# Layer-norm statistics spread over attention steps on VectorE, and a shorter wait between two layers, in a fused transformer kernel

## The chip, the cores and the metric

The kernel runs on one core of one Trainium2 chip. The metric is the device time in microseconds (us) of one execution. TensorE multiplies matrices, VectorE does element-wise work and reductions, ScalarE exponentials and copies, GpSimd masks and indirect transfers, and SyncE starts most DMA transfers. Each engine works through its own instructions in their order and waits on semaphores for the others.

## What is computed

The input x has 16 sequences of 256 tokens of 128 features. Four parts follow each other, each added to x:

```python
x = x + attn_a(layernorm(x))   # 16 heads of 8, causal softmax
x = x + ffn(layernorm(x))      # 8 experts of 128 -> 512 -> 128, the best 2 for each token
x = x + attn_b(layernorm(x))   # 16 heads of 8, no mask, a scale and shift worked out for each head
x = x + ffn(layernorm(x))
```

The layer norm subtracts the mean of a token's 128 features and divides by sqrt(variance + 1e-5).

## The kernel before, in words

x stays in on-chip memory as 32 blocks of 128 tokens, two blocks to a sequence. The kernel has four stages: attention "A", a feed-forward stage, attention "B", a second feed-forward stage. "Layer A" and "layer B" are called l = 0 and l = 1 in the code.

**An attention layer is a pipeline of steps j.** Step j (`pipeline`, `pe_step`, `dve_step` and so on) projects sequence j, computes the scores of sequence j-2 for their row maxima, the transposed scores and exponentials of sequence j-3, and the output of sequence j-4. Each step goes through 16 slots h, one for each head. In slot h TensorE writes the scores of head h (L355, in layer A with a mask matmul L386) into one of two banks psS, and VectorE reduces the bank to the row maxima (mx, L671). TensorE's scores of slot h wait for the maximum of slot h-2, `after(pe, s["mx"], 16 * bS + h - 1)`, so VectorE can be at most about two slots late before TensorE stands still. Beside the maxima VectorE has other duties in fixed slots: xs, the normalised input of step j, in slot 0; the lower part of a maximum in slots 2 and 10; the softmax division in slots 5 and 12; the residual in slots 9 and 15; in layer A splits in slots 11 and 14.

**Hooks put further work between the slots.** `dve_beside` issues work for VectorE at the end of a given slot. Part of it are the layer-norm statistics of a group of blocks, by `dve_ln_at`. It cuts them into one call for each value of its argument h: count/2 calls with two `bn_stats` each (one for each block), two calls with half of the `bn_aggr` each, and a last call, the root (`dve_ln_root`): 13 small instructions, each of which waits for the one before, that give 1/sqrt(variance + eps) by an integer seed and three Newton steps. VectorE does nothing else during the root. Where `dve_ln_at` is called:

- layer A, step 5: blocks 16 to 31 of the input, for the inputs xs from step 8 on
- layer A, step 13: blocks 0 to 15, for the feed-forward stage
- layer B, step 7: blocks 16 to 31, for the inputs xs from step 8 on
- layer B, step 14: blocks 0 to 15, for the second feed-forward stage
- step 18 of both layers and the feed-forward stages, which stay as they are

In layer B `dve_combine_1` also adds the experts' outputs of blocks 16 to 31 to x, four blocks at a time: in slot 4 of steps 4, 5 and 6, and in slot 2 of step 7.

**A feed-forward stage** goes through 71 tiles of 128 tokens (`tile_loop`). The result of a tile is copied by VectorE to ysb (L1417), and a DMA started by SyncE stores it to eo in DRAM. GpSimd gathers the rows of eo later, and waits itself for the stores (`pool_gather`). After the first feed-forward stage TensorE and ScalarE call `ffn_over` ahead of layer B, which begins with step 2, since the projections of sequences 0 and 1 were made beside the last tiles.

Of the kernel before, what the change touches and what calls it, by code (L numbers as in the profile page):

```python
# [23 lines left out]
HALF = NBLK // 2  # L24
SIZE = (16, 16)
BASE = (0, SIZE[0])
QUADS = (SIZE[0] // 4, SIZE[1] // 4)
TILES = 2 * NBLK + E - 1
# [40 lines left out]
def build(nc, A, out):  # L69
    with ExitStack() as ctx:  # L70
# [35 lines left out]
        part = sb("part", [P, 2, 3, T], BF16)  # L106
# [82 lines left out]
        s_lnA = sem("s_lnA")  # L189
# [3 lines left out]
        s_ln = [sem("s_ln0"), sem("s_ln1"), sem("s_ln2"), sem("s_ln3")]  # L193
# [4 lines left out]
        s_lnB = sem("s_lnB")  # L198
# [696 lines left out]
        def tiles_done(p, l, count):  # L895

            return 16 * (l * ((TILES + 1 - p) // 2) + (count + 1 - p) // 2)

        def ffn_over(eng, l):

            eng.wait_ge(f_sem["y"], TILES * (l + 1))
            for i in range(2):
                eng.wait_ge(f_st[i], tiles_done(i, l, TILES))

        LG_COPIES = (0, 1, 3, 4)

# [725 lines left out]
        def dve_beside(l):  # L1632
            n = 2 * l

            def hook(dve, j, h):
                x1 = (LA, LB)[l].s["x1"]
                if l == 0 and j == 1 and h == 1:
                    dve.wait_ge(s_xrest, 16)
                    dve_ln_stats(dve, 4, HALF, s_lnA)
                    dve.wait_ge(s_lnA, 2)  # L1640
                if l == 0 and j == 5 and h == 0:
                    dve.wait_ge(s_xlast, 16)
                if l == 0 and j == 5:
                    dve_ln_at(dve, h, HALF, HALF, s_lnA, 3)
                if l == 0 and j == 1 and h == 15:
                    dve.wait_ge(s_mset, 2 * RING)
                    nc.vector.memset(half[0:1, 0, :], -0.5).then_inc(s_half, 1)
                    nc.vector.memset(half[0:1, 1, :], 1.5).then_inc(s_half, 1)
                    dve.wait_ge(s_cst, 16)
                    nc.vector.memset(onesb[:], 1.0).then_inc(s_half, 1)  # L1650
                    nc.vector.tensor_copy(triu[:], cst[:, CST_TRIU:CST_TRIU + P]).then_inc(s_half, 1)
                if l == 1 and (j, h) in ((4, 4), (5, 4), (6, 4), (7, 2)):
                    dve_combine_1(dve, 0, j - 4)
                if l == 1 and (j, h) == (2, 12):
                    dve_route_part(dve, 1, 2)
                if l == 1 and j == 7:
                    dve_ln_at(dve, h, SIZE[0], SIZE[1], s_lnB, 3)
                if l == 0 and j == 13:
                    if h == 0:
                        dve.wait_ge(x1, HALF)  # L1660
                    dve_ln_at(dve, h, 0, HALF, s_ln[0], 1)
                if l == 0 and j == 14:
                    if h % 4 == 1:
                        dve_tokens(dve, 0, h - 1, h + 3)
                if l == 0 and j == 15:
                    if h == 9:
                        dve_logits(dve, 0, 0, QUADS[0], 1)
                    if h in (10, 11):
                        dve_route_part(dve, 0, h - 10)
                    if h == 15:  # L1670
                        dve_counts(dve, 0)
                if l == 0 and j == 16 and h < 4:
                    dve_route_part(dve, 0, h + 4)
                if l == 1 and j == 14:
                    if h == 0:
                        dve.wait_ge(x1, SIZE[0])
                    dve_ln_at(dve, h, 0, SIZE[0], s_ln[2], 1)
                if l == 1 and j == 16 and h in (8, 9):
                    if h == 8:
                        dve_logits(dve, n, 0, QUADS[0], LG_COPIES[n] + 1)  # L1680
                    dve_route_part(dve, n, h - 8)
                if l == 1 and j == 16 and h == 11:
                    dve_counts(dve, n)
                if l == 1 and j == 16 and 12 <= h < 16:
                    dve_route_part(dve, n, h - 8)
                if j == 18 and h == 15:
                    dve_route_part(dve, n, 8)
                    dve_route_part(dve, n, 2)
                if j == 18:
                    if h == 0:  # L1690
                        dve.wait_ge(x1, NBLK - 4)
                    dve_ln_at(dve, h, SIZE[0], NBLK - 4 - SIZE[0], s_ln[n + 1], 1)
                    if 10 <= h < 14:
                        dve_tokens(dve, n + 1, SIZE[0] + 3 * (h - 10), SIZE[0] + 3 * (h - 9))
                if j == 19 and h == 10:
                    dve_logits(dve, n + 1, 0, QUADS[1] - 1, LG_COPIES[n + 1] + 1)
                    dve_pick(dve, n + 1, 0, 0, NBLK - 4 - BASE[1])
                if j == 19 and h == 13:
                    dve_pick(dve, n + 1, 1, 0, NBLK - 4 - BASE[1])
                if l == 0 and j == 18 and h == 15:  # L1700
                    dve_setup(dve, LB)
            return hook
# [155 lines left out]
```

## Time and profile before

| | |
|---|---|
| median of 3 runs | 1166.69 us (1163.05 to 1168.38) |
| profiled execution | 1166.68 us, of which the span of the trace is 1164.9 us |
| TensorE matmuls busy | 1029.9 us (88%) |
| VectorE busy | 755.5 us (65%) |
| ScalarE busy | 672.4 us (58%) |
| GpSimd busy | 525.5 us (45%) |
| TensorE's granted clock, mean | 0.92 |

A span is the time from the first to the last event of the trace. The granted clock is 1.00 at 2.4 GHz and 0.50 at 1.2 GHz; a value between them is the mean of a stretch that has both. A shared number of busy engines says little here: the stages have different limits, so the prediction reads single steps.

A step is taken from the start of VectorE's xs (L583) to the next one. In a row of a window stand: its bounds, its length, then for TensorE's matmuls, TensorE's weight loads, VectorE, ScalarE and GpSimd the busy time with the number of instructions in brackets, then TensorE's granted clock, the DMA engines' share and GB/s. In a row of a timeline stand: start, duration, engine, line, operation, what is written and read, shapes, count, and in square brackets the idle time of the engine just before it and what ended it. Instructions of one engine overlap a little.

### The profile page before, as it was taken

What the parts mean: (1) busy time and instruction counts of PE and PEld (TensorE: products, weight loads), DVE (VectorE), ACT (ScalarE), POOL (GpSimd) and SP (SyncE); (2) the same over time, 40 slices, a digit from 0 to 9 for tenths busy, and PEclk for the clock granted to TensorE, in tenths of its full rate; (3) what the DMA queues carried; (4) which work ended last, traced back from release to release, by engine and by line L of the source; (5) the groups of instructions that cost most, each with busy time, mean ns of one, the idle gap of its engine ahead of it and who ended that gap; (6) DMA issues with size and microseconds to landing.
All of it is one profiled execution on the core that took longest, in us unless ns stands there. A gap on an engine that the chain in (4) does not pass through costs nothing.

```text
span 1164.9 us, 28879 instructions
## 1 busy us (share of the span) xinstructions
PE 1029.9 (88%) x9290; PEld 716.6 (62%) x9290; DVE 755.5 (65%) x2322; ACT 672.4 (58%) x1399; POOL 525.5 (45%) x980
## 2 busy tenths in 40 slices
PE   2998999897989999999798979999888799999990
PEld 1444555453468989999443434444443589999990
DVE  4687778877777333456777888888877663334442
ACT  2365676663644545556277858897757445455550
POOL 2243444332742610344687736455736436004455
PEclk9998999996989999999778979998888899999995
DMA  6446544562235878887544323343221469778873
GB/s 152 104 114 138 116 110 99 151 181 57 54 118 174 271 233 236 260 255 236 125 111 104 101 56 85 89 107 84 65 49 44 130 191 280 227 242 256 272 225 109
DMA packets 201723, 175.03 MB, mean 150 GB/s; under 512 B 19812, under 2 KB 160616, under 8 KB 201576
## 3 DMA queue, kind: packets, MB, share of 16 engines
q1 hardware_dynamic: 193384, 156.41, 49.1%
q0 software_dynamic: 8192, 16.79, 4.8%
q8 instruction: 76, 1.25, 0.5%
q14 instruction: 71, 0.58, 0.2%
HBM read 122.99 MB, written 50.14 MB: 149 GB/s over the span
## 4 chain that ended last, share of the span: by engine, by line
PE 60%; DVE 11%; issue 6%; POOL 5%; DMA 4%; SPq 3%; ACT 1%; POOLq 0%; ACTq 0%; DVEq 0%
PE psS L1358 9%; PE psT L1365 9%; PE psO L321 8%; PE psS L355 7%; PE psO L1381 4%; PE psN L1381 4%; DVE mx L671 4%; PE psS L386 3%; PE psT L363 3%; POOL xn L1259 3%; PE psM L276 2%; PE psN L328 2%; DMA eo<-ysb 2%; PE psN L337 1%; PE psM L1346 1%
## 5 line engine op out<-in xcount | busy, mean ns | idle before, releaser
L671 DVE TENSOR_REDUCE mx<-psS 128x3 f32<-128x384 f32 (+1 forms) x512 | 311.4, 617 | 119.5 <-PE psS L386 61.8
L355 PE MATMUL psS<-kst,qst 48*128 48x256 bf16 (+1 forms) x1024 | 201.7, 286 | 46.4 <-DVE mx L671 33.2
L558 ACT ACTIVATE pT<-psT,scb 128x512 f32<-128x512 f32 x256 | 193.9, 777 | 43.2 <-PE psT L363 40.7
L363 PE MATMUL psT<-qst,kst 50*128 50x256 bf16 (+1 forms) x1024 | 194.7, 278 | 4.6 <-DMA qst<-scr_m 2.2
L1422 DVE TENSOR_TENSOR hT<-sg,psT 128x512 f32<-128x512 f32 x142 | 97.5, 686 | 154.4 <-PE psT L1365 127.7
L1245 POOL DMA_INDIRECT xg<-xn,slot x128 | 123.1, 962 | 131.3 <-DVE ysb L1417 72.1
L1358 PE MATMUL psS<-xTt,wgc 128*128 128x128 f32 x1136 | 153.7, 279 | 5.7 <-issue 5.3
L355 PEld LDWEIGHTS psS<-kst,qst 48*128 48x128 bf16 x1024 | 66.2, 97 | 146.0 <-DVE mx L671 68.2
L1365 PE MATMUL psT<-xTt,wuc 128*128 128x128 f32 x1136 | 152.2, 278 | 1.5 <-DMA wuc<-in_L_ffn_Wu 1.4
L790 POOL TENSOR_SCALAR_AFFINE_SELECT pT<-pT 128x256 f32<-128x256 f32 x224 | 90.6, 412 | 133.0 <-ACT pT L553 131.8
L553 ACT ACTIVATE pT<-psT 128x384 f32<-128x384 f32 x256 | 122.9, 490 | 46.1 <-PE psT L363 35.9
L1358 PEld LDWEIGHTS psS<-xTt,wgc 128*128 128x128 f32 x1136 | 140.0, 194 | 9.2 <-issue 8.5
L1365 PEld LDWEIGHTS psT<-xTt,wuc 128*128 128x128 f32 x1136 | 140.0, 194 | 2.3 <-DMA wuc<-in_L_ffn_Wu 2.3
L321 PE MATMUL psO<-pT,vp 128*32 128x256 f32 (+1 forms) x2048 | 141.0, 399 | 0.4 <-ACT pT L558 0.3
L1259 POOL DMA_INDIRECT pT<-eo,slot x64 | 60.4, 944 | 175.9 <-DVE ysb L1417 105.7
L1401 ACT ACTIVATE sg<-psS 128x512 f32<-128x512 f32 x142 | 84.7, 596 | 83.0 <-PE psS L1358 82.9
L1409 ACT ACTIVATE wdc<-wd 128x512 f32 x142 | 89.5, 630 | 52.1 <-issue 48.7
L321 PEld LDWEIGHTS psO<-pT,vp 128*32 128x32 f32 x2048 | 57.6, 118 | 55.5 <-issue 29.1
L1392 ACT ACTIVATE xTt<-psM 128x128 f32<-128x128 f32 x142 | 39.3, 277 | 70.5 <-PE psM L1346 70.3
L386 PE MATMUL psS<-trib,identb 128*128 128x256 bf16 x256 | 77.5, 303 | 0.0
L1381 PE MATMUL psN<-wdc,hT 128*128 128x128 f32 x576 | 76.2, 275 | 1.0 <-DVE ysb L1417 1.0
L1381 PE MATMUL psO<-wdc,hT 128*128 128x128 f32 x560 | 74.3, 276 | 0.5 <-DVE ysb L1417 0.5
(225 smaller groups left out, 1595.1 us busy)
## 6 DMA issues: line engine op xcount, KB each, us to landing
wgc<-in_L_ffn_Wg SPq DMA_DIRECT2D x142, 256.0 KB, 3.1
wuc<-in_L_ffn_Wu SPq DMA_DIRECT2D x142, 256.0 KB
scr_part<-part SPq DMA_DIRECT2D x128, 128.0 KB, 2.1
qst<-scr_part SPq DMA_DIRECT2D x64, 192.0 KB, 3.7
kst<-scr_part SPq DMA_DIRECT2D x64, 192.0 KB, 4.7
xin<-xg SPq DMA_DIRECT2D x142, 64.0 KB
eo<-ysb SPq DMA_DIRECT2D x142, 64.0 KB
scr_part<-part SPq DMA_DIRECT2D x32, 192.0 KB, 1.9
```

The source lines that it names most:

```text
L321: last = nc.tensor.matmul(psO[q // 2][32 * i:32 * i + 32, o0 + dst[0]:o0 + dst[1]], vp[r][:, kb, h, :], pT[:, h % 8, src[0]:src[1]], start ...
L355: return nc.tensor.matmul(ps[:, c0:c0 + n], q_[r64, t, q0], k_[r64, t, 0:n], start=(half == 0), stop=True, skip_group_check=True)
L363: return nc.tensor.matmul(ps[:, c0:c0 + T - q0], k_[m64, t, half * P:half * P + P], q_[m64, t, q0:T], start=(half == 0 or not L.causal), s ...
L386: last_s = nc.tensor.matmul(psS[par][:, 0:3 * P].rearrange("p (a k) -> p a k", a=3)[:, 0:3:2, :], identb[:], trib[:].unsqueeze(1).to_broad ...
L553: nc.scalar.activation(pT[:, g % 8, 0:cols], psT[g % 2][:, 0:cols], ACT.Exp, scale=float(HD) ** -0.5).then_inc(s["exp"], 1)
L558: nc.scalar.activation(pT[:, g % 8, 0:cols], psT[g % 2][:, 0:cols], ACT.Exp, scale=scb[r][:, 0, i:i + 1], bias=scb[r][:, 1, i:i + 1]).then ...
L671: nc.vector.tensor_reduce(mx3[:, u, 0:n, pos:pos + 1].rearrange("p a b -> p (a b)"), psS[h % 2][:, 0:kcols(L)].rearrange("p (a k) -> p a k ...
L1245: nc.gpsimd.indirect_dma_start(xg, bass.IndirectOffsetOnAxis(ap=slot[g][:, i, k:k + 1], axis=0), xn[:, BASE[g] + k, :], None).then_inc(r_s ...
L1358: last = nc.tensor.matmul(psS[p][:, cols], wgc[n % FETCH][:, cols], xTt[n % FETCH][:], start=True, stop=True, skip_group_check=True)
L1365: last = nc.tensor.matmul(psT[p][:, cols], wuc[n % FETCH][:, cols], xTt[n % FETCH][:], start=True, stop=True, skip_group_check=True)
L1381: last = nc.tensor.matmul(psY[p][:, 0:P], hT[(n0 + k - 2) % FETCH][:, hb, :], wdc[(n0 + k - 2) % FETCH][:, hb * P:(hb + 1) * P], start=(hb ...
L1422: nc.vector.tensor_tensor(out=hT[(n0 + k) % FETCH][:].rearrange("p a c -> p (a c)"), in0=sg[p][:], in1=psT[p][:], op=ALU.mult).then_inc(f[ ...
```

## The change

**Statistics.** The calls of `dve_ln_at` are dealt over two steps, and in layer B, blocks 16 to 31, over two groups of eight blocks with a root each:

| statistics | before | after |
|---|---|---|
| layer A, blocks 16 to 31 | step 5, slots 0 to 10 | `bn_stats` in the even slots of step 4, `bn_aggr` in slots 0 and 1 and the root in slot 2 of step 5 |
| layer A, blocks 0 to 15 | step 13, slots 0 to 10 | the same way in steps 12 and 13 |
| layer B, blocks 16 to 23 | step 7, slots 0 to 10 (16 blocks) | `bn_stats` in slots 0, 4, 8, 12 of step 6, the rest in slots 0 to 2 of step 7 |
| layer B, blocks 24 to 31 | (same) | `bn_stats` in slots 0, 4, 8, 12 of step 9, the rest in slots 0 to 2 of step 10 |
| layer B, blocks 0 to 15 | step 14, slots 0 to 10 | even slots of step 13, slots 0 to 2 of step 14 |

The last call of `dve_combine_1` moves from slot 2 of step 7 to slot 4 of step 8.

**The wait.** `ffn_over` no longer waits for the stores of the tiles (f_st), only for the copies to ysb (y). TensorE's and ScalarE's work of layer B doesn't read what the stores write; GpSimd's gathers keep their own waits.

```diff
         def ffn_over(eng, l):
 
             eng.wait_ge(f_sem["y"], TILES * (l + 1))
-            for i in range(2):
-                eng.wait_ge(f_st[i], tiles_done(i, l, TILES))
...
-                if l == 0 and j == 5 and h == 0:
+                if l == 0 and j == 4 and h == 0:
                     dve.wait_ge(s_xlast, 16)
-                if l == 0 and j == 5:
-                    dve_ln_at(dve, h, HALF, HALF, s_lnA, 3)
+                if l == 0 and j == 4 and h % 2 == 0:
+                    dve_ln_at(dve, h // 2, HALF, HALF, s_lnA, 3)
+                if l == 0 and j == 5 and h < 3:
+                    dve_ln_at(dve, HALF // 2 + h, HALF, HALF, s_lnA, 3)
...
-                if l == 1 and (j, h) in ((4, 4), (5, 4), (6, 4), (7, 2)):
-                    dve_combine_1(dve, 0, j - 4)
+                if l == 1 and (j, h) in ((4, 4), (5, 4), (6, 4), (8, 4)):
+                    dve_combine_1(dve, 0, min(j - 4, 3))
...
-                if l == 1 and j == 7:
-                    dve_ln_at(dve, h, SIZE[0], SIZE[1], s_lnB, 3)
-                if l == 0 and j == 13:
-                    if h == 0:
-                        dve.wait_ge(x1, HALF)
-                    dve_ln_at(dve, h, 0, HALF, s_ln[0], 1)
+                for part, (first, times) in enumerate(((6, 3), (9, 4))):
+                    lo, count = SIZE[0] + part * SIZE[1] // 2, SIZE[1] // 2
+                    if l == 1 and j == first and h % 4 == 0:
+                        dve_ln_at(dve, h // 4, lo, count, s_lnB, times)
+                    if l == 1 and j == first + 1 and h < 3:
+                        dve_ln_at(dve, count // 2 + h, lo, count, s_lnB, times)
+                if l == 0 and j == 12 and h == 0:
+                    dve.wait_ge(x1, HALF)
+                if l == 0 and j == 12 and h % 2 == 0:
+                    dve_ln_at(dve, h // 2, 0, HALF, s_ln[0], 1)
+                if l == 0 and j == 13 and h < 3:
+                    dve_ln_at(dve, HALF // 2 + h, 0, HALF, s_ln[0], 1)
...
-                if l == 1 and j == 14:
-                    if h == 0:
-                        dve.wait_ge(x1, SIZE[0])
-                    dve_ln_at(dve, h, 0, SIZE[0], s_ln[2], 1)
+                if l == 1 and j == 13 and h == 0:
+                    dve.wait_ge(x1, SIZE[0])
+                if l == 1 and j == 13 and h % 2 == 0:
+                    dve_ln_at(dve, h // 2, 0, SIZE[0], s_ln[2], 1)
+                if l == 1 and j == 14 and h < 3:
+                    dve_ln_at(dve, SIZE[0] // 2 + h, 0, SIZE[0], s_ln[2], 1)
```

VectorE's instructions from slot 12 of step 4 of layer A to slot 2 of step 5, after the change (mx is a maximum, bn_stats appear as BN_STATS):

```order
L934 BN_STATS bn<-x 128x6 x2
L671 TENSOR_REDUCE mx<-psS 128x3
L705 TENSOR_TENSOR vp<-psM,b_wideA 128x16x8 x2
L671 TENSOR_REDUCE mx<-psS 128x3
L627 TENSOR_TENSOR part<-rest,part 128x2x256
L934 BN_STATS bn<-x 128x6 x2
L671 TENSOR_REDUCE mx<-psS 128x3
```

Before the change the same place had no BN_STATS; the first of them stood behind the xs of step 5:

```order
L583 TENSOR_SCALAR xs<-x,mean_rstd 128x128 x2
L936 BN_STATS bn<-x 128x6 x2
L671 TENSOR_REDUCE mx<-psS 128x3
L936 BN_STATS bn<-x 128x6 x2
L671 TENSOR_REDUCE mx<-psS 128x3
```

So two pairs more stand ahead of the last maxima of step 4 (a third stands in slot 10).

VectorE's instructions from slot 1 to slot 3 of step 7 of layer B, before the change (L1289 adds the experts' outputs):

```order
L936 BN_STATS bn<-x 128x6 x2
L671 TENSOR_REDUCE mx<-psS 128x2
L633 SCALAR_TENSOR_TENSOR mrow<-psN,neg_shift,mrow 8x256
L1289 SCALAR_TENSOR_TENSOR x<-xn,wgt,x 128x128 x8
L936 BN_STATS bn<-x 128x6 x2
L671 TENSOR_REDUCE mx<-psS 128x2
```

And the same slots after it, in step 7 and again in step 10, where nothing of the kind stood before (the root begins with L880):

```order
L583 TENSOR_SCALAR xs<-x,mean_rstd 128x128 x2
L939 BN_AGGR mean_rstd<-bn 128x2 x4
L671 TENSOR_REDUCE mx<-psS 128x2
L688 COPY scb<-psM 128x32
L690 COPY neg_shift<-psM 8x2
L939 BN_AGGR mean_rstd<-bn 128x2 x4
L671 TENSOR_REDUCE mx<-psS 128x2
L633 SCALAR_TENSOR_TENSOR mrow<-psN,neg_shift,mrow 8x256
L880 TENSOR_SCALAR nwt<-mean_rstd 128x8
```

The root now stands between the maxima of slots 2 and 3, where the experts' outputs were added before, instead of between those of slots 10 and 11.

## Rows read from the trace of the kernel before

**Rows 1.** The page of the kernel before: busy time of TensorE.

```profile
PE 1029.9 (88%) x9290; PEld 716.6 (62%) x9290; DVE 755.5 (65%) x2322; ACT 672.4 (58%) x1399; POOL 525.5 (45%) x980
```

**Rows 2.** Windows, one per step; columns as described above.

```profile
62.62:78.53 15.91, 15.39 (x174) 8.14 (x172) 12.57 (x33) 11.23 (x27) 7.10 (x17) 1.00 0.45 102
78.53:99.16 20.63, 16.98 (x174) 8.55 (x172) 18.87 (x78) 11.61 (x27) 7.08 (x17) 0.92 0.74 173
212.74:233.89 21.15, 17.50 (x172) 8.53 (x171) 19.01 (x79) 11.62 (x27) 7.09 (x17) 0.85 0.66 188
647.97:668.69 20.72, 18.13 (x172) 8.62 (x168) 17.13 (x50) 16.06 (x33) 14.00 (x32) 0.92 0.41 101
668.69:697.63 28.94, 22.10 (x160) 9.69 (x160) 23.72 (x94) 15.95 (x32) 11.13 (x28) 0.72 0.25 61
697.63:716.13 18.50, 18.03 (x184) 8.92 (x176) 15.01 (x41) 16.50 (x34) 9.88 (x28) 0.98 0.39 89
786.32:803.86 17.54, 16.94 (x172) 8.35 (x168) 14.84 (x41) 15.72 (x33) 9.84 (x28) 1.00 0.41 93
803.86:829.89 26.03, 22.00 (x172) 9.96 (x168) 21.46 (x86) 16.27 (x33) 16.09 (x36) 0.74 0.26 63
```

**Rows 3.** Timeline of VectorE, end of step 4, layer A.

```profile
72.22 0.56 DVE L671 TENSOR_REDUCE mx<-psS 128x3 f32<-128x384 f32 x1 [0.84 <-PE psS L386]
```

**Rows 4.** Timeline of TensorE, idle time in brackets, layer A.

```profile
77.92 0.23 PE L355 MATMUL psS<-kst,qst 48*128 48x128 bf16 x1 [0.45 <-DVE mx L671]
...
80.88 0.23 PE L355 MATMUL psS<-kst,qst 48*128 48x128 bf16 x1 [0.21 <-DVE mx L671]
...
93.69 0.23 PE L355 MATMUL psS<-kst,qst 48*128 48x128 bf16 x1 [2.67 <-DVE mx L671]
```

**Rows 5.** Timeline of VectorE, steps 7 and 14, layer B.

```profile
671.72 2.29 DVE L1289 SCALAR_TENSOR_TENSOR x<-xn,wgt,x 128x128 f32<-128x128 f32 x8
...
804.37 0.47 DVE L936 BATCH_NORM_STATS2 bn<-x 128x6 f32<-128x128 f32 x2
...
815.77 0.63 DVE L941 BATCH_NORM_AGGREGATE mean_rstd<-bn 128x2 f32<-128x6 f32 x8
...
819.60 0.15 DVE L880 TENSOR_SCALAR nwt<-mean_rstd 128x16 f32<-128x16 f32 x1
...
822.29 1.29 DVE L671 TENSOR_REDUCE mx<-psS 128x2 f32<-128x512 f32 x2
```

**Rows 6.** Timeline of TensorE, steps 6, 7 and 14, layer B.

```profile
656.06 0.33 PE L333 MATMUL psN<-ident,on 128*128 128x128 f32 x1 [2.26 <-DVE on L643]
...
675.18 0.39 PE L355 MATMUL psS<-kst,qst 48*128 48x256 bf16 x1 [2.61 <-DVE mx L671]
...
805.49 0.28 PE L355 MATMUL psS<-kst,qst 48*128 48x256 bf16 x1 [0.61 <-DVE mx L671]
...
806.63 0.28 PE L355 MATMUL psS<-kst,qst 48*128 48x256 bf16 x1 [0.39 <-DVE mx L671]
```

**Rows 7.** Windows over stretches of the lower granted clock.

```profile
94.33:97.74 3.41, 3.41 (x29) 1.51 (x21) 2.64 (x8) 2.36 (x6) 0.81 (x2) 0.50 0.61 178
...
674.60:681.40 6.80, 6.22 (x37) 2.58 (x37) 4.72 (x17) 2.38 (x5) 3.55 (x17) 0.50 0.64 116
807.70:818.00 10.30, 10.03 (x62) 3.90 (x61) 8.05 (x38) 5.43 (x12) 7.01 (x21) 0.50 0.41 81
```

**Rows 8.** Timeline of VectorE: the last copy of the first feed-forward stage.

```profile
563.90 0.28 DVE L1417 COPY ysb<-psN 128x128 f32<-128x128 f32 x1
```

**Rows 9.** Timeline of TensorE: the first scores of layer B.

```profile
566.09 0.61 PE L355 MATMUL psS<-kst,qst 48*128 48x256 bf16 x4 [3.76 <-DMA eo<-ysb]
```

**Rows 10.** The chain that ended last, at the same place.

```profile
564.37 1.63 DMA eo<-ysb
```

**Rows 11.** Tile kst from 550 to 575 us: DMA issues to it.

```profile
L819 SPq DMA_DIRECT2D kst<-scr_part x4: 432/472/536, 556.1 to 572.4; - x4
DMA to landing us min/median/max: 4.1/4.8/5.4
```
## The prediction

> **What bounds the kernel now.** The page comes first: TensorE's matmuls are busy for 88% of the span [rows 1]. Then the windows of single steps, which are what the change touches. A step without statistics takes 15.91 us in layer A and 17.54 us in layer B, and TensorE is busy for all but 0.52 and 0.60 us of them; VectorE idles 3.3 and 2.7 us. The steps with statistics are longer: +4.72 us (step 5, layer A), +5.24 us (step 13), +11.40 us (step 7, layer B, with the experts' outputs), +8.49 us (step 14); step 8 is 0.96 us over [rows 2]. So at most some 31 us are at stake, and the question is what of them the new places give back.
>
> Two losses make up each of these. One is TensorE's idle time: length less busy time rises by 3.13 us in step 5, 3.13 us in step 13, 6.24 us in step 7 and 3.43 us in step 14. The other is that the same matmuls take longer: +1.59, +2.11, +5.16 and +5.06 us, with a granted clock of 0.92, 0.85, 0.72 and 0.74 [rows 2]. The timeline of TensorE shows where the idle time is. In step 5 one wait on a maximum has 2.67 us, and it ends when the root does; the statistics in slots 0 and 1 left only 0.21 us [rows 4]. In layer B they left 0.61 and 0.39 us [rows 6], and a half-clock stretch of 10.3 us followed; after the 2.67 us wait one of 3.4 us, after the 2.61 us wait of step 7 one of 6.8 us [rows 6, 7].
>
> **Cost of the pieces.** Two bn_stats take 0.47 us (0.4 us taken, since neighbours overlap), eight bn_aggr 0.63 us, the root 822.29 - 819.60 = 2.69 us, the experts' outputs 2.29 us [rows 5]. The root is one uninterrupted piece before and after, and has the same 13 instructions for 8 blocks as for 16. That is my main argument: the change spreads what was cheap and keeps whole what was dear, and layer B, blocks 16 to 31, gets a second root. What would a root cost in slot 2? Step 7 shows it: there the experts' outputs and one pair of statistics, 2.29 + 0.4 = 2.69 us, stood between the maxima of slots 2 and 3, and TensorE waited 2.61 us [rows 5, 6]. A root at slot 2 is the same length at the same place.
>
> **What a half clock costs.** From windows: in step 14 the clock of 0.74 means 2 x 0.26 x 26.03 = 13.5 us at half, for 5.06 us of longer matmuls, 0.37 us for each. In step 7 it is 2 x 0.28 x 28.94 = 16.2 us for 5.16 us, 0.32 for each; in step 5 it is 3.3 us for 1.59 us, 0.48 for each [rows 2]. I use 0.32 to 0.37 in layer B. The Trainium skill (TensorE: Matmul & The Clock Gate, section Terms) gives the loss as throttled time x (1 - K/N), that is 0.5 for each microsecond at half; the trace is below it where VectorE's waits overlap, and by the rule step 14 would have lost 6.8 us to the clock instead of 5.1.
>
> **Layer A, steps 4 and 5.** In step 4 VectorE starts the maximum of slot 10 after an idle 0.84 us, and from there works without a pause into the next step, where TensorE waits 0.45 us for it [rows 3, 4]. Pairs in slots 0 to 8 fall into idle time. Those of slots 10, 12 and 14 lie in the unbroken run, so 3 x 0.4 = 1.2 us go to TensorE's wait (bounds 0 and 1.2). A wait of 0.45 + 1.2 us in one place may bring a half-clock stretch of its own: 0 or 1.6 us, 0.8 taken. Step 5: two half groups of bn_aggr in slots 0 and 1 are 2 x 0.23 us longer than the pairs they replace, the root costs 2.67 us as before and a stretch at half clock 1.6 us; I take the 4.7 us of before again (4.0 to 5.5). Sum of both: +2.0 us.
>
> **Layer A, steps 12 and 13.** The same, but the half clock after the root was already longer there (0.85 against 0.92 [rows 2]), so I add no second stretch: +1.2 us (0 to 3).
>
> **Layer B, steps 6 to 10.** Before: 11.40 + 0.96 = 12.4 us over the normal steps. After: step 6 has pairs at slots 0 and 4, where VectorE was late already (a 2.26 us wait [rows 6]), +0.8 us. Step 7: waits of 0.61 + 0.39 + 2.61 us [rows 6], of which a normal step has some 0.4, so 3.2 us, and 6.8 us of half clock [rows 7] x 0.32 = 2.2 us: 5.4 us. Step 8 gets the experts' outputs in slot 4, as step 6 has them: 20.72 - 17.54 = 3.2 us [rows 2] (2 to 3.2, since part of step 6's is GpSimd's gathering). Step 9: one pair exposed, 0.4 us. Step 10: a root as in step 7, 5.4 us. Sum 15.2 us against 12.4: +2.8 us (-2 to +7).
>
> **Layer B, steps 13 and 14.** Eight pairs, 3.2 us, go into a step in which VectorE idles 2.7 us [rows 2]. Slots 0 and 2 cost 0.6 us; of slots 10 to 14 I let 0.8 us (0 to 1.2) arrive in step 14. There: 0.8 + 0.61 + 0.39 + 2.61 us, 0.5 us since bn_aggr is longer than a pair, less 0.4: 4.5 us. Half clock between 2.2 us (6.8 us as in step 7) and 3.8 us (10.3 us x 0.37 [rows 7]), 3.0 taken. 0.6 + 4.5 + 3.0 = 8.1 us against 8.49: -0.4 us (-3 to +2).
>
> **The boundary.** VectorE's last copy starts at 563.90 and takes 0.28 us [rows 8], so it ends at 564.18; the scores start at 566.09 after 3.76 us of idle time, ended by the store [rows 9], which in the chain takes 1.63 us [rows 10]. Without the wait the scores start about 1.8 us earlier. What else must be there: kst, issued from 556.1 on and landed at most 5.4 us later [rows 11], even with half a microsecond for its second piece 562.0 at the latest. Behind it VectorE's xs and GpSimd's chain start with the same step, so the gain stays: -1.8 us (-1.9 to 0). The Trainium skill (DMA: Bandwidth & Descriptors, "Anatomy of one DMA") puts a transfer's fixed cost at about 2.0 us; by that the gain would be 2.2 us, the trace shows less.
>
> **Sum.** -1.8 + 2.0 + 1.2 + 2.8 - 0.4 = +3.8 us on the profiled execution of 1166.68 us, which lies at the median of the runs (1166.69): 1170.5 us. GpSimd's normalising in step 14 starts earlier, but nothing of the next step waits for it.
>
> **Rivals.**
> 1. Shorter stretches: every root brings only 3.4 us of half clock (1.3 us), as in step 5, and none at the step ends. Against my sum that saves 0.8 + 0.3 in steps 4 and 5, 2.1 - 1.3 in step 13, 2 x 0.9 in steps 7 and 10 and 3.0 - 1.3 in step 14, 5.4 us: 1165 us. For it: with statistics spread, TensorE enters the root without small waits before it. Against it: bn_aggr sits there instead. 25%.
> 2. Clearly faster: TensorE holds its full clock through the roots. Then of the four places only idle time is left: 1.2 + 3.1 - 4.7, the same with 5.2, 0.8 + 3.2 + 2.3 + 0.4 + 3.2 - 12.4, 0.6 + 4.5 - 8.5, and the boundary: -0.4 - 0.9 - 2.5 - 3.4 - 1.8 = -9 us, 1158 us. Against it: the waits of 2.67 and 2.61 us, and even those of 0.61 and 0.39 us together, had a half-clock stretch behind them [rows 4, 6, 7]. It decides if TensorE's waits stay under that of 0.61 + 0.39 us. 17%.
> 3. Slower: each root of layer B brings 10.3 us of half clock and each step end in layer A one more stretch. That is 0.8 + 1.6 us more in layer A, 2 x 1.6 in steps 7 and 10 and 0.8 in step 14 of layer B, +6.4 us: 1177 us. It decides once lags of the step end and the root fall together, as in steps 13 and 14. 18%.
> 4. The wait at the boundary is only replaced (by ScalarE, GpSimd or the clock): 1172 us, with the forecast. Its share of the forecast's 40% is a fourth.
>
> **How the numbers follow.** 40% for 1167 to 1173, with 1170.5 the likeliest; the others as given. Two in ten left out: 1157 to 1178 us. A measurement here can tell about 0.5%, 5.8 us, from no change. Faster than 1160.9: rival 2 and a little of rival 1, 0.20. Slower than 1172.5: rival 3 and the upper part of the forecast, 0.27. Same: 0.53.
>
> **What would show it.** Right: waits of about 2.6 us on a maximum in slot 5 of steps 5 and 13 (A), 7, 10 and 14 (B); a wait of 1 to 2 us at the end of steps 4 and 12; step 10 near 23 us; scores of layer B under 0.3 us behind the last copy. Wrong: steps 5, 7, 10 and 14 with a clock near 1.00, or waits there well below 2.6 us, or step 13 of layer B at 17.5 us.

## The result: 0.66% slower

The changed kernel takes 1172.64 us (median of 5 runs, 1169.91 to 1174.10) against 1164.48 us for the kernel before in the same comparison (5 runs, 1163.05 to 1168.38). The ratio is 1.0066, with a 95% interval of 1.0043 to 1.0088, so it is slower by 5 to 10 us. The prediction had 1170.5 us, a range of 1157 to 1178 us and 27% for slower by over 0.5%. Its profiled execution took 1169.91 us, with a span of 1168.2 us; that is its fastest run, so the single trace shows less than the medians do.

The page after, its first lines (span, then busy time of each engine):

```profile
span 1168.2 us, 28898 instructions
PE 1028.0 (88%) x9290; PEld 716.3 (61%) x9290; DVE 757.7 (65%) x2335; ACT 673.2 (58%) x1399; POOL 526.3 (45%) x980
```

TensorE is busy as long as before [rows 1]. VectorE has 13 instructions more, one root. The loss is in how the steps fit together, and the windows by step show it (bounds, length, then busy times, and the third number from the end is TensorE's granted clock). Layer A, steps 4, 5, 12, 13 and 14, then layer B, steps 6, 7, 8, 9, 10, 13 and 14:

```profile
62.04:79.14 17.10, 15.85 (x174) 8.22 (x172) 15.38 (x50) 11.19 (x27) 7.51 (x17) 1.00 0.43 106
79.14:99.88 20.74, 16.89 (x174) 8.64 (x172) 16.18 (x62) 11.57 (x27) 7.16 (x17) 0.92 0.63 147
195.99:213.06 17.07, 15.82 (x174) 8.22 (x172) 15.37 (x49) 11.19 (x27) 7.49 (x17) 1.00 0.44 106
213.06:234.40 21.34, 18.33 (x174) 9.18 (x172) 16.46 (x62) 11.57 (x27) 7.17 (x17) 0.84 0.58 151
234.40:255.35 20.95, 17.71 (x178) 9.36 (x177) 17.09 (x49) 12.44 (x29) 7.27 (x17) 0.92 0.68 175
647.04:667.20 20.16, 18.12 (x172) 8.87 (x168) 18.65 (x57) 16.08 (x33) 13.94 (x32) 0.92 0.39 102
667.20:689.90 22.70, 19.13 (x172) 9.20 (x168) 17.75 (x62) 16.13 (x33) 9.90 (x28) 0.85 0.33 79
689.90:709.79 19.89, 18.02 (x172) 8.63 (x168) 17.07 (x49) 16.07 (x33) 9.89 (x28) 0.91 0.34 83
709.79:728.18 18.39, 16.89 (x172) 8.43 (x168) 16.47 (x49) 15.81 (x33) 9.86 (x28) 1.00 0.34 89
728.18:751.11 22.93, 19.03 (x172) 9.05 (x168) 17.75 (x62) 16.13 (x33) 9.89 (x28) 0.85 0.29 72
786.22:807.09 20.87, 18.71 (x173) 8.88 (x169) 17.72 (x58) 16.23 (x33) 9.91 (x28) 0.92 0.34 78
807.09:830.13 23.04, 18.93 (x172) 9.17 (x168) 18.36 (x70) 15.95 (x33) 15.70 (x36) 0.85 0.31 71
```

Against [rows 2]: step 7 of layer B fell from 28.94 to 22.70 us and step 14 from 26.03 to 23.04 us. But the step ahead of each group now costs something (17.10 for 15.91 us in layer A, 20.87 for 17.54 us in layer B), step 5 of layer A is no shorter (20.74 for 20.63 us), and step 10 of layer B, where nothing stood, is 22.93 us long.

The timeline of TensorE after the change has the waits behind the roots, which now stand in slot 2 (idle time in brackets). Layer A, end of step 4, step 5 and step 14; layer B, first scores, steps 7, 10 and 14:

```profile
78.53 0.23 PE L355 MATMUL psS<-kst,qst 48*128 48x128 bf16 x1 [0.84 <-DVE mx L671]
...
85.77 0.23 PE L355 MATMUL psS<-kst,qst 48*128 48x128 bf16 x1 [2.66 <-DVE mx L671]
...
243.88 0.34 PE L363 MATMUL psT<-qst,kst 50*128 50x256 bf16 x1 [1.65 <-DMA qst<-scr_m]
...
565.16 0.61 PE L355 MATMUL psS<-kst,qst 48*128 48x256 bf16 x4 [1.85 <-DVE ysb L1415]
...
673.62 0.39 PE L355 MATMUL psS<-kst,qst 48*128 48x256 bf16 x1 [2.17 <-DVE mx L671]
...
734.60 0.39 PE L355 MATMUL psS<-kst,qst 48*128 48x256 bf16 x1 [2.50 <-DVE mx L671]
...
814.12 0.39 PE L355 MATMUL psS<-kst,qst 48*128 48x256 bf16 x1 [2.14 <-DVE mx L671]
```

2.66 us in step 5 is the 2.67 us of [rows 4], eight slots earlier; step 13 of layer A has such a wait of 2.50 us. The boundary wait fell from 3.76 [rows 9] to 1.85 us and is now ended by VectorE's copy. The wait of 1.65 us in step 14 was not there before.

### The profile page after: what moved, and what is told of

Same layout as the page of the kernel before. It is cut to its first block, busy times and chain, and to the rows that moved or that the text cites. A ratio compares the mean times of both kernels' runs of the same rounds, so it can differ in the third digit from the quotient of the medians.

```text
span 1168.2 us, 28898 instructions
## 1 busy us (share of the span) xinstructions
PE 1028.0 (88%) x9290; PEld 716.3 (61%) x9290; DVE 757.7 (65%) x2335; ACT 673.2 (58%) x1399; POOL 526.3 (45%) x980
## 4 chain that ended last, share of the span: by engine, by line
PE 59%; DVE 13%; POOL 9%; issue 8%; DMA 6%; SPq 3%; ACT 2%; POOLq 0%; ACTq 0%; DVEq 0%
PE psS L1356 9%; PE psT L1363 9%; PE psO L321 8%; PE psS L355 7%; PE psO L1379 4%; PE psN L1379 4%; DVE mx L671 4%; POOL xn L1257 4%; PE psS L386 3%; PE psT L363 3%; PE psM L276 3%; POOL prow L745 2%; PE psN L328 2%; POOL part L758 1%; PE psN L337 1%
## 5 line engine op out<-in xcount | busy, mean ns | idle before, releaser
L355 PE MATMUL psS<-kst,qst 48*128 48x256 bf16 (+1 forms) x1024 | 199.1, 282 | 50.2 <-DVE mx L671 39.7
L558 ACT ACTIVATE pT<-psT,scb 128x512 f32<-128x512 f32 x256 | 194.4, 778 | 46.2 <-PE psT L363 43.5
L363 PE MATMUL psT<-qst,kst 50*128 50x256 bf16 (+1 forms) x1024 | 192.2, 275 | 5.5 <-DMA qst<-scr_m 2.7
L553 ACT ACTIVATE pT<-psT 128x384 f32<-128x384 f32 x256 | 123.0, 491 | 53.1 <-PE psT L363 43.6
```

Of the source, the lines that this page charges most:

```text
L355: return nc.tensor.matmul(ps[:, c0:c0 + n], q_[r64, t, q0], k_[r64, t, 0:n], start=(half == 0), stop=True, skip_group_check=True)
L363: return nc.tensor.matmul(ps[:, c0:c0 + T - q0], k_[m64, t, half * P:half * P + P], q_[m64, t, q0:T], start=(half == 0 or not L.causal), s ...
L553: nc.scalar.activation(pT[:, g % 8, 0:cols], psT[g % 2][:, 0:cols], ACT.Exp, scale=float(HD) ** -0.5).then_inc(s["exp"], 1)
L558: nc.scalar.activation(pT[:, g % 8, 0:cols], psT[g % 2][:, 0:cols], ACT.Exp, scale=scb[r][:, 0, i:i + 1], bias=scb[r][:, 1, i:i + 1]).then ...
```

## The experiments

"Below" and "above" are taken from the ratio to the kernel before, run on the same chip in the same comparison. 1% is 11.7 us.

**1. Only the shorter wait.**

```diff
             eng.wait_ge(f_sem["y"], TILES * (l + 1))
-            for i in range(2):
-                eng.wait_ge(f_st[i], tiles_done(i, l, TILES))
```

> Only the shorter wait at the boundary; the statistics stay as before. Theory T (the terms of the prediction): the scores of layer B start some 2 us earlier and the gain stays, so 1.8 to 2.2 us below the kernel before. Rival R (the loss is at the boundary: starting earlier costs more later, in steps 2 to 6 or in the second feed-forward stage): equal to the kernel before, or above it by up to 5 us.

1161.90 us against 1164.96 us, ratio 0.9971 (0.9953 to 0.9988): 1.4 to 5.5 us faster. Theory T holds, R falls. From the xs of sequence 1 to that of step 2 it takes 27.3 us in this trace and 26.9 in the changed kernel's, 28.7 to 29.1 us in the traces that keep the wait: 1.8 us less by the means. In the changed kernel the first scores start 0.06 us behind VectorE's last copy.

**2. Only the statistics.** The changed kernel with the two lines of the wait put back.

> Only the statistics dealt over the steps; the boundary waits for the stores as before. Theory T: all of the loss is here, so about 2 us above the changed kernel, that is 8 to 11 us above the kernel before. Rival R: between the kernel before and the changed one, 0 to 4 us above before.

1176.01 us, ratio 1.0099 (1.0069 to 1.0128): 8 to 15 us slower. The dealt statistics are the loss, and the wait takes some 2 to 4 us off it (1.8 us by the traces, 3.8 us by the two ratios).

**3. Only layer A.** The kernel before with the dealt calls of steps 4, 5, 12 and 13.

> Only the two groups of layer A are dealt over two steps (4 and 5, 12 and 13). Theory T: +1.2 us for each of steps 4 and 12 and what step 14 lost in the changed kernel's trace (2.2 us), less 1.3 us in step 6: 2.5 to 3.5 us above the kernel before. Rival R: no loss in layer A that lasts, within 1 us of the kernel before.

1170.08 us, ratio 1.0041 (1.0019 to 1.0064): 2 to 7 us slower, about half of the loss; rival R falls. Its step 5 shows how much the clock adds by chance:

```profile
78.55:102.36 23.81, 20.83 (x174) 9.64 (x172) 16.36 (x62) 11.81 (x27) 7.24 (x17) 0.72 0.53 128
```

The same instructions took 20.74 us at a clock of 0.92 in the changed kernel and 23.81 us at 0.72 here; TensorE idles less (2.98 against 3.85 us), its matmuls take 3.9 us longer. So two traces of the same instructions can differ by 3 us in one step, and the steps of a single trace have to be read with that in mind.

**4. Only blocks 16 to 31 of layer B.**

> Only blocks 16 to 31 in layer B are dealt as in the change: two groups, two roots, the last experts' outputs in step 8. Theory T: step 7 loses about 6 us of its length, steps 8, 9 and 10 gain 1.4, 0.8 and 5.4, so 0.8 to 2.8 us above the kernel before, and step 10 is near 23 us. Rival R: a second root of eight blocks is cheap, step 10 under 19 us and the whole some 4 us below the kernel before.

1169.92 us, ratio 1.0042 (1.0023 to 1.0060): 3 to 7 us slower, where I expected 0.8 to 2.8 us; step 10 is 22.96 us long. A root of 8 blocks is not cheap, and rival R falls. The excesses of experiments 3 and 4, 0.41% and 0.42%, add to most of the 0.99% of experiment 2.

The next four ran on another chip, on which the kernel before takes 1229.08 us (33 runs, 1223.62 to 1238.06), mostly because its feed-forward stages are longer (301.0 and 365.1 us in the trace of experiment 6, 276.4 and 333.1 us in that of the kernel before). Ratios hold within that comparison. Steps of layer A and steps 9 to 13 of layer B are as long as in the traces so far where they have the same work (15.88 and 17.55 us). The changed kernel did not run on this chip: where it is the measure, its ratio of 1.0066 is taken over from the first comparison.

**5. The roots of the changed kernel in four pieces.**

```diff
-                if l == 0 and j == 5 and h < 3:
-                    dve_ln_at(dve, HALF // 2 + h, HALF, HALF, s_lnA, 3)
+                if l == 0 and j == 5 and h in (0, 1, 2, 4, 6, 8):
+                    dve_ln_at(dve, HALF // 2 + (0, 1, 2, 4, 6, 8).index(h), HALF, HALF, s_lnA, 3, True)
```

and the same in steps 13 of layer A and 7, 10 and 14 of layer B. A piece is the start with its integer seed (3 instructions), or one Newton step (3), the last one with the copy.

> The changed kernel, with the five roots of its dealt groups cut into four pieces of 3 to 4 instructions, in slots 2, 4, 6 and 8 instead of all in slot 2. Theory T (the root's unbroken 2.7 us late in the slots is what TensorE waits for; a piece of 0.65 us falls into VectorE's idle time): each of the five waits of 2.1 to 2.7 us and most of the half clock behind it go, some 3.5 us each, so 14 to 20 us below the changed kernel, and steps 5 (layer A) and 10 (layer B) are under 18.5 and 20 us. Rival S (VectorE's added work costs the same wherever it stands): within 3 us of the changed kernel.

Ratio 0.9993 (0.9973 to 1.0014). The changed kernel stands at 1.0066, so the pieces take off some 8 us, not 14 to 20. In layer A the waits on the root are gone as theory T has it: steps 5 and 13 are 17.86 us long at full clock. But step 6 then took 18.86 us, against 17.01 us in the changed kernel, with a wait of 1.45 us on a transfer (qst<-scr_m), so over steps 4 to 6 only 1.0 us of the 2.9 us is left; experiment 10 comes back to this. In layer B steps 7 and 10 stay long (the rows are step 5 of layer A, then 7 and 10 of layer B):

```profile
79.14:97.00 17.86, 15.69 (x174) 8.18 (x172) 16.12 (x63) 11.43 (x27) 7.07 (x17) 1.00 0.72 164
...
701.72:722.13 20.41, 16.82 (x172) 8.15 (x168) 19.24 (x63) 16.47 (x33) 9.89 (x28) 1.00 0.33 80
761.78:784.46 22.68, 19.33 (x172) 8.96 (x168) 19.27 (x63) 16.58 (x33) 9.92 (x28) 0.85 0.32 73
```

VectorE is busy for 19.27 us in step 10, where the changed kernel had 17.75 us with the same work: two instructions of the root take 1.15 and 0.90 us there, and 0.17 us elsewhere. Experiment 8 shows what runs beside them. Steps 7 and 10 have the same waits of TensorE to 0.03 us (0.64, 0.40, 0.50 and 1.55 us in step 7, which has one of 0.20 us more), and yet step 7 kept the full clock and step 10 did not.

**6. The roots of the kernel before in four pieces, in slots 10 to 13.**

> The kernel before, with only its four roots cut into the same four pieces, in slots 10, 11, 12 and 13 of the same step; everything else as before. Theory T (the place counts as much as the length: behind slot 10 VectorE works without a pause anyway): TensorE still waits for most of the 2.7 us, in several smaller waits, so 0 to 5 us below the kernel before. Rival U (only the unbroken length counts): 10 to 15 us below the kernel before.

Ratio 1.0000 (0.9974 to 1.0025). Theory T holds, rival U falls. TensorE's waits in step 5 are now several: 0.43, 0.84 and

```profile
96.22 0.21 PE L355 MATMUL psS<-kst,qst 48*128 48x128 bf16 x1 [1.56 <-DVE mx L671]
```

which is 2.8 us together, against one of 2.67 us [rows 4]. Behind slot 10 VectorE has no idle time to hide the root in, and cutting it there gives little in layer A: steps 5 and 13 take 19.91 and 20.01 us, 0.7 and 1.1 us less than in [rows 2]. Cutting it and placing it in slots 2 to 8 gives 3 us in a step (experiment 5). Steps 7 and 14 of layer B took 25.67 and 23.23 us in this trace, 3.3 and 2.8 us less than in [rows 2], and the whole still gains nothing. There is no trace of the kernel before on this chip, so where that is lost again stays open.

**7. The pairs of bn_stats in slots 1 to 8 instead of the even slots** (2 to 9 in layer B, step 13).

```diff
-                if l == 0 and j == 4 and h % 2 == 0:
-                    dve_ln_at(dve, h // 2, HALF, HALF, s_lnA, 3)
+                if l == 0 and j == 4 and 1 <= h <= 8:
+                    dve_ln_at(dve, h - 1, HALF, HALF, s_lnA, 3)
```

> The changed kernel, with the eight pairs of bn_stats of steps 4 and 12 (layer A) in slots 1 to 8 instead of the even slots, and those of step 13 (layer B) in slots 2 to 9; aggregation and root as in the change. Theory T (the pairs of slots 10, 12 and 14 lie in the unbroken run and cost 0.4 us each, those of slots 3 to 9 fall into idle time): steps 4 and 12 are back at 15.9 us, step 13 at 17.5 to 18.5 us, 3 to 6 us below the changed kernel. Rival S: no difference.

Ratio 1.0016 (1.0000 to 1.0033), against 1.0066 for the change: about 6 us less. Theory T holds. Steps 4 and 12 of layer A and 13 of layer B:

```profile
62.22:78.44 16.22, 15.57 (x175) 8.14 (x172) 15.37 (x50) 11.24 (x27) 7.14 (x17) 1.00 0.45 104
195.67:211.81 16.14, 15.52 (x174) 8.16 (x172) 15.37 (x50) 11.24 (x27) 7.11 (x17) 1.00 0.41 101
826.62:844.72 18.10, 16.72 (x172) 8.24 (x168) 17.73 (x58) 15.77 (x33) 9.83 (x28) 1.00 0.39 90
```

VectorE's busy time is that of the changed kernel (15.37 and 17.73 us); only the slots differ, and 0.9 us a step in layer A and 2.8 us in layer B are gone. The pairs in slot 0 and from slot 10 on were the cost; the run moved both and does not part them.

**8. Everything in the idle slots.** The kernel before with the shorter wait, and all four groups in slots 3 to 9: for layer A

```diff
+            if j == first and 3 <= h < 9:
+                dve_ln_at(dve, h - 3, lo, count, done, times, True)
+            if j == first + 1 and h in (3, 4, 6, 8):
+                dve_ln_at(dve, 6 + (3, 4, 6, 8).index(h), lo, count, done, times, True)
+            if j == first + 2 and h in (3, 5, 7, 8):
+                dve_ln_at(dve, 10 + (3, 5, 7, 8).index(h), lo, count, done, times, True)
```

with first = 4 and 11; blocks 0 to 15 of layer B so from step 12 on, blocks 16 to 31 in two groups in steps 6, 7 and 10, 11, and `dve_combine_1` in halves in slots 4 and 7 of steps 4, 5, 8 and 9.

> The kernel before with the shorter wait of the change, and all statistics and roots of the four groups dealt over two or three steps, with nothing in slots 0 to 2 and 10 to 15: pairs and bn_aggr in slots 3 to 9, the roots in four pieces in slots 3 to 9 of a later step, the experts' outputs of steps 4, 5, 8 and 9 in two halves in slots 4 and 7. Theory T: the steps with statistics are within 1 us of the normal ones (15.9 and 17.5 us); of the 30 us that they had over them 20 to 27 go, and 2 us at the boundary: 1136 to 1145 us. Rival S: the same work, so at most the 3 us of the boundary.

Ratio 0.9924 (0.9895 to 0.9953): 6 to 13 us faster, not the 22 to 29 us that I expected with the boundary. Steps 4, 5, 12 and 13 of layer A are at 16.01, 17.11, 16.22 and 16.32 us, but others are not. Step 5 of layer B takes 29.22 us, where the other three traces of this chip have 25.5 to 28.0 us; why is open. Two losses can be read. First, steps 6 and 14 of layer A take 20.03 and 22.05 us and wait for the same transfer, for 2.48 us in step 6 and in step 14 so:

```profile
237.86 0.28 PE L363 MATMUL psT<-qst,kst 50*128 50x256 bf16 x1 [2.79 <-DMA qst<-scr_m]
```

Second, step 11 of layer B takes 21.43 us. VectorE's last piece of the root and GpSimd's splits of the projections at the same time, from the two timelines:

```profile
787.18 0.16 DVE L937 SCALAR_TENSOR_TENSOR nwt<-nwt 128x8 f32<-128x8 f32 x1
787.37 1.01 DVE L938 TENSOR_TENSOR nwt<-nwt 128x8 f32<-128x8 f32 x1
788.42 0.17 DVE L939 SCALAR_TENSOR_TENSOR nwt<-nwt 128x8 f32<-128x8 f32 x1
788.62 0.90 DVE L941 COPY mean_rstd<-nwt 128x8 f32<-128x8 f32 x1
```

```profile
787.18 1.18 POOL L758 TENSOR_TENSOR rest<-qk,part 128x512 f32<-128x512 f32 x1
788.44 1.05 POOL L758 TENSOR_TENSOR part<-rest,zero 128x512 bf16<-128x512 f32 x1
```

The 8-column multiplication took 1.01 us, not 0.17, and ended at 788.38, where GpSimd's instruction ended at 788.36; the copy ended at 789.52 with GpSimd's next one at 789.49. The maximum behind the copy came late, and TensorE waited 1.62 us for it. Experiments 9 to 12 take these two losses apart, 9 to 11 on a chip where the kernel before takes 1163.95 us, 12 on one where it takes 1165.33 us.

**9. The pieces ahead of the split,** in slots 3, 5, 6 and 7. The edit does this in both layers, though it is meant for layer B.

> The kernel of the idle slots, with the root's pieces of layer B in slots 3, 5, 6 and 7, ahead of GpSimd's four split instructions, instead of up to slot 9. Theory V (a small VectorE instruction that begins while GpSimd splits is held until GpSimd's instruction ends, 1.0 us instead of 0.17): the two long instructions in each of steps 7, 11 and 14 and the waits of 1.4 to 1.6 us behind them go, 1.5 to 4 us for each step, 4 to 10 us below the kernel of the idle slots, that is 13 to 20 us below the kernel before. Rival (chance, or the pieces themselves): steps 7 and 11 stay above 20 us.

1149.61 us, ratio 0.9899 (0.9867 to 0.9931). This is the faster chip, so the comparison with experiment 8 goes by ratios: 0.25% less, with intervals that overlap; it is not shown as a gain, and the 4 to 10 us expected did not come. Nor did the run test theory V, since what held VectorE did not go: GpSimd began its split with the last piece in slot 7, and one multiplication took 1.13 us and the copy 1.01 us in each of the three steps. Steps 7, 11 and 14 took 22.22, 19.38 and 19.43 us, against 20.45, 21.43 and 19.05 us in experiment 8. Steps 7 and 11 have the same instructions and nearly the same waits (0.39 and 1.51 us, 0.38 and 1.51 us); the clock makes the difference:

```profile
660.74:682.96 22.22, 19.45 (x172) 9.13 (x168) 18.79 (x54) 16.29 (x33) 9.87 (x28) 0.85 0.40 100
737.40:756.78 19.38, 16.58 (x172) 8.06 (x168) 18.60 (x54) 15.86 (x33) 9.87 (x28) 1.00 0.36 84
```

The last run moves that piece.

**10. The same, with SyncE's large transfers spread.**

```diff
-            if j == 5:
-                for e in (2 * point, 2 * point + 1):
+            if j in (3, 4, 5, 6) and point == 3:
+                for e in (2 * (j - 3), 2 * (j - 3) + 1):
...
-            if j in (13, 14):
+            if 7 <= j <= 14 and point == 3:
                 sp.wait_ge(s_zero, 1)
-                part8 = 4 * (j - 13) + point
+                part8 = j - 7
```

> The same kernel, and the large transfers that SyncE starts beside layer A are spread: the eight loads of the experts' weights over steps 3 to 6 instead of step 5, the eight zero fills of the token buffer over steps 7 to 14 instead of 13 and 14, always at the end of SyncE's step. Theory W (what steps 5 and 13 gain comes back in steps 6 and 14, because the exchange of the row maxima waits behind these transfers): TensorE's waits of 1.5 to 2.8 us on that exchange in steps 6 and 14 go, another 4 to 8 us. Rival: the exchange is slow for another reason, no difference.

1141.62 us, ratio 0.9812 (0.9785 to 0.9840), 10 us below experiment 9 by the ratios, with intervals that don't meet. Steps 5, 6, 13 and 14 of layer A, which took 17.17, 19.10, 16.71 and 21.78 us in experiment 9:

```profile
78.73:94.95 16.22, 15.42 (x174) 8.12 (x172) 14.42 (x53) 11.25 (x27) 7.13 (x17) 1.00 0.57 140
94.95:111.45 16.50, 15.58 (x174) 8.21 (x172) 15.04 (x46) 11.36 (x27) 7.11 (x17) 1.00 0.49 116
207.29:223.70 16.41, 15.44 (x174) 8.13 (x172) 15.13 (x46) 11.25 (x27) 7.09 (x17) 1.00 0.49 135
223.70:241.48 17.78, 16.19 (x177) 8.87 (x176) 16.85 (x50) 12.27 (x29) 7.26 (x17) 1.00 0.49 119
```

Together 66.9 us against 74.8. The wait on the exchange of the row maxima (qst<-scr_m) was 1.56 us in step 6 and 2.48 us in step 14; it is 0.41 us in step 6 now and gone in step 14, and so is the half clock. Theory W holds: these transfers were what the exchange waited for. Whether it stood behind them in SyncE's queue or shared the DMA engines with them no run parts.

**11. The change as it was, with the same spread of the transfers.**

> The changed kernel with the same spread of the transfers and nothing else. Theory W: step 14 comes down from 21 us by 1.5 to 3 us and step 6 by some 1 us, so 2 to 5 us below the changed kernel, 3 to 6 us above the kernel before. Rival: as the changed kernel, 8 us above the kernel before.

1171.71 us, ratio 1.0063 (1.0034 to 1.0092): no difference from the change is seen, where I expected 2 to 5 us; the two intervals leave room for a gain of some 4 us. Steps 13 and 14 of layer A:

```profile
215.54:239.34 23.80, 20.83 (x174) 9.62 (x172) 16.38 (x63) 11.82 (x27) 7.20 (x17) 0.72 0.34 86
239.34:257.11 17.77, 16.18 (x177) 8.88 (x176) 16.84 (x49) 12.26 (x29) 7.26 (x17) 1.00 0.46 116
```

Step 14 gained 3.2 us and lost its wait on the exchange, as expected, but step 13 with its root had a clock of 0.72 and lost 2.5 us. Step 6 did not gain (18.92 us). Whether the clock of step 13 follows from the moved transfers or is the chance seen in experiments 3 and 9 is open; one trace does not tell it.

**12. The last piece in slot 6** (slots 3, 4, 5 and 6), again in both layers.

> The kernel with the moved transfers, and the root's four pieces of layer B in slots 3, 4, 5 and 6: the last piece stood in slot 7, where GpSimd's split began with it. Theory V: no small VectorE instruction of 1.0 us is left in steps 7, 11 and 14, TensorE's waits of 1.5 us behind them go, and these steps fall from 19.4 to 20.8 us to 18 to 19 us: 3 to 6 us less, 22 to 28 us below the kernel before. Rival: pieces in four neighbouring slots bring waits of their own, no gain or a loss of up to 3 us.

1143.86 us against 1165.33 us, ratio 0.9823 (0.9799 to 0.9847): no gain over experiment 10 is seen, where I expected 3 to 6 us. What held VectorE is gone, as expected; the last piece in step 7:

```profile
663.48 0.16 DVE L937 SCALAR_TENSOR_TENSOR nwt<-nwt 128x8 f32<-128x8 f32 x1
663.67 0.17 DVE L938 TENSOR_TENSOR nwt<-nwt 128x8 f32<-128x8 f32 x1
663.87 0.17 DVE L939 SCALAR_TENSOR_TENSOR nwt<-nwt 128x8 f32<-128x8 f32 x1
664.08 0.17 DVE L941 COPY mean_rstd<-nwt 128x8 f32<-128x8 f32 x1
```

Step 7 took 18.51 us. Steps 11 and 14 took 19.79 and 20.12 us with smaller waits (0.55 to 0.62 us each) but a clock of 0.91 and 0.92, where experiment 10 had 20.81 and 19.44 us. Over the three steps that is 58.4 us against 61.1 us. But the edit moves the pieces of layer A too, into neighbouring slots, and there steps 6 and 13, 16.50 and 16.41 us in experiment 10, took longer:

```profile
94.28:112.78 18.50, 17.13 (x174) 8.48 (x172) 15.23 (x46) 11.62 (x27) 7.09 (x17) 0.91 0.49 103
208.94:226.05 17.11, 15.64 (x174) 8.21 (x172) 15.19 (x46) 11.35 (x27) 7.14 (x17) 1.00 0.47 130
```

In these traces the 2.7 us lost in layer A are as much as layer B gained. A run with slots 3 to 6 in layer B alone was not made, so what the release of VectorE is worth to the whole stays open.

## Why the prediction was right

The sum's terms, against the difference between the mean of the traces that have the edit and of those that don't, out of the kernels before and after and experiments 1 to 4:

| term | predicted | measured in the traces |
|---|---|---|
| layer A, steps 4 and 5 | +2.0 us | +1.6 us with step 6 (steps 4 to 6: 54.9, 55.6, 57.8 against 54.9, 54.8, 53.8) |
| layer A, steps 12 and 13 | +1.2 us | +3.7 us with step 14 (steps 12 to 14: 59.4, 59.3, 60.3 against 55.8, 55.8, 56.4) |
| layer B, steps 6 to 10 | +2.8 us | +2.3 us (104.1, 106.0, 104.3 against 103.3, 103.1, 101.0) |
| layer B, steps 13 and 14 | -0.4 us | +0.4 us (43.9, 44.1 against 43.6, 44.2, 43.5, 43.1) |
| boundary | -1.8 us | -1.8 us |
| sum | +3.8 us | +6.2 us, by runs +7.7 us (5.0 to 10.2) |

The traces of one group differ by up to 3 us in a row, so a single term is known to 1 or 2 us only. In the pair before and after alone, steps 4 to 6 are equal (54.9 us) and steps 6 to 10 differ by 0.8 us.

**The main argument held:** the root, which was left whole, was the dear part. Its wait of 2.1 to 2.7 us turned up in slot 5 of all five steps (2.17 and 2.14 us in steps 7 and 14 of layer B, a little under the forecast). The second root of layer B cost 5.4 us (22.93 against 17.55 us), as the prediction had it, and in its parts: 3.3 us of added idle time and 2.1 us of longer matmuls, against 3.2 and 2.2 us. Step 4 of layer A grew by the forecast 1.2 us (17.10 - 15.91 us), and experiment 7 took 0.9 us of it out again. For layer A the change itself and experiments 5 and 6 together show that neither the unbroken length nor the place alone decides: whole in slot 2 the root costs the same wait, in pieces behind slot 10 it costs nearly what it did, in pieces in slots 2 to 8 the step is 2 us over a normal one and keeps its clock. For layer B this is not shown as clearly, because GpSimd's work beside the pieces (experiment 5) and the open point of experiment 6 come in.

**The term that was mis-sized** is layer A, steps 12 and 13, +1.2 us forecast and +3.7 us measured with step 14: 2.1 us in steps 12 and 13 themselves and 1.5 us in step 14. I had left step 14 out, since nothing of the change is in it. In the kernel before a half-clock stretch reached into it and it took 18.78 us; after the change it took 20.95 us, of which 1.65 us are a wait on the exchange of the row maxima that had not shown in that step. Experiments 10 and 11 spread SyncE's zero fills, and in both this wait is gone. The wait of TensorE at the end of step 4 was 0.84 us, a little under the 1 to 2 us that I expected, and the half-clock stretch that I had half counted there never came: steps 4 and 12 had a clock of 0.99 or 1.00 in all the traces with this order.

**Step 13 of layer B** was dearer than its term (3.3 us over a normal step, not 0.6), and step 14 cheaper (5.5 us over, not 7.5): their sum came out right, 0.8 us off, by two errors of opposite sign, which is luck. Step 13 idled 1.6 us more than a normal step and its matmuls took 1.8 us longer (clock 0.92), which the term left out. Step 14 had 3.5 us of added idle time instead of 4.5, and 2.0 us of longer matmuls instead of 3.0.

**How near the number is.** 1170.5 us lies 2.1 us from the measured 1172.64 us, but that flatters the sum: it was added to an execution of 1166.68 us, and the kernel before then had a median of 1164.48 us. The forecast change was +3.8 us and the measured one +7.7 us. The sign and the main terms were right, the loss came out about twice as large, and more chance had been given to a change too small to tell (53%) than to the loss that was measured (27%).

**The boundary.** The Trainium skill (DMA: Bandwidth & Descriptors, "Anatomy of one DMA") gives the 2.0 us that the prediction sets beside its -1.8 us for the path of transfers that GpSimd starts. This store was started by SyncE and took 1.63 us [rows 10], and the gain in the traces was 1.8 us, not 2.2 us. By its runs experiment 1 gained 3.4 us (1.4 to 5.5), which does not tell the two apart.

**The rivals.** By the trace of the changed kernel, rival 1 (3.4 us of half clock for each root) fell in four of the five steps: a clock of 0.85 over 22.70 us is 2 x 0.15 x 22.70 = 6.8 us at half in step 7. Only step 5 of layer A fits it (3.3 us), and its other half, no half clock at the ends of steps 4 and 12, came true. Rival 2 (full clock through the roots) is excluded: steps 5, 7, 10, 13 and 14 had 0.92, 0.85, 0.85, 0.84 and 0.85. Rival 3 (10.3 us stretches in layer B) did not come: steps 7, 10 and 14 had 6.8 to 6.9 us at half. Rival 4 falls: the boundary's wait was not replaced by another, and experiment 1 has the gain alone. What stays open is the spread between runs of one kernel, 4 to 17 us here; the traces differ in which steps fall into half-clock stretches, and I have no experiment that sets it.

## What to carry to other kernels

In this kernel spreading work paid only where the pieces that stalled the waiting engine got smaller, and only in slots where the busy engine really idled. So read from the timeline both the longest unbroken piece and the stretches without a pause, then place. A kernel with the same statistics and the shorter wait, the root in four pieces, everything in slots 3 to 9 and the large transfers spread (experiment 10) is 1.9% faster than the one before (1141.62 us), while the even spread with a whole root was 0.7% slower. And when a slow step gets faster, look one step on: transfers that it covered can come up there, as in steps 6 and 14 of layer A. Where an edit meant for one place also reaches another, read both: in experiment 12 the gain in layer B and the loss in layer A were of one size.

## What the runs showed of the hardware that was not expected

**VectorE held by GpSimd.** Multiplications and copies of 128x8 or 128x16 elements took 0.75 to 1.15 us instead of 0.17 us when GpSimd ran an instruction of 128x512 elements, and ended within 0.04 us of it (experiments 5, 8, 9 and 10, two in each step). Reductions from PSUM beside such GpSimd work took 0.67 to 0.69 us, no longer than elsewhere. Small instructions that began with GpSimd's or up to 0.03 us ahead of it kept 0.17 us; but in experiments 9 and 10 the held multiplication began 0.07 to 0.09 us ahead, so who has to begin first is not shown. The Trainium skill (GPSIMD Engine Reference, section 1, Specifications) says that GpSimd shares its SBUF interfaces with VectorE and contends with VectorE instructions that have two SBUF inputs or run in a 2-port mode; the multiplication has two such inputs, so the trace agrees. The copy has one input, and whether it ran in a 2-port mode no trace here shows. TensorE waited 1.5 to 1.6 us behind each of these places (experiments 8, 9 and 10); what that is worth to the whole is open, as said at experiment 12.

**Small waits and the clock.** Waits of 0.64 and 0.40 us ahead of a wait of 2.50 us (step 10 of layer B, the changed kernel) go with a clock of 0.85; a single wait of 0.84 us in a step of layer A left it at 1.00. But the waits do not settle it: steps 7 and 11 of experiment 9, and steps 7 and 10 of experiment 5, have nearly the same waits, and in each pair one step has a clock of 0.85 and the other of 1.00.

**Another chip.** The kernel before took 1229.08 us on the chip of experiments 5 to 8 and 1164 to 1165 us in the other comparisons, with the same lengths of the normal attention steps (15.88 and 17.55 us).
